# Group convolutions of a fused graph network: steps over the tiles that hold graphs (58), in place of four tiles in each of 16 batches

## The reference, cut to what matters

```python
GROUPS = [list(range(25)), [0, 1, 2, 3, 4, 5, 6, 7, 8], [0, 9, 10, 11, 12, 13, 14], [6, 7, 8, 12, 13, 14], [3, 4, 5, 9, 10, 11]]
def _graph_conv(x, adj, W, b):
    n = adj.shape[-1]
    A = adj + jnp.eye(n, dtype=adj.dtype)
    deg = jnp.sum(A, axis=-1)
    deg_safe = jnp.where(deg == 0, 1.0, deg)
    dinv = jnp.where(deg == 0, 0.0, deg_safe ** (-0.5))
    norm_adj = dinv[:, :, None] * A * dinv[:, None, :]
    support = jnp.einsum('bnd,de->bne', x, W)
    out = jnp.einsum('bnm,bme->bne', norm_adj, support) + b
    return jax.nn.relu(out)
...
    for g, idx_list in enumerate(GROUPS):
        idx = jnp.asarray(idx_list)
        x_g = x[:, idx, :]
        adj_g = adj[:, idx][:, :, idx]
        h = _graph_conv(x_g, adj_g, W1[g], b1[g])
        out_g = _graph_conv(h, adj_g, W2[g], b2[g])
        fused = fused.at[:, idx, :].add(norm_w[g] * out_g)
```

## Time and profile before

| | |
|---|---|
| time, median of 3 runs (lowest to highest) | 1251.85 us (1251.16 to 1252.07) |
| time of the profiled execution | 1249.13 us |
| its span, first to last instruction | 1247.3 us |
| mean granted TensorE clock | 0.937 of full speed |
| PE, DVE, ACT, POOL busy over the span | 91%, 82%, 78%, 61% |
| end of the first stage in the trace | 237.2 us |

### The profile page before, as it was taken

How to read it: one execution, slowest core, us unless ns; L and a number is a source line. 1 busy time by engine, 2 the same in 40 slices (tenths; PEclk the granted TensorE clock), 3 DMA queues, 4 the chain that set the end, 5 groups by cost and what they waited for, 6 DMA issues and landing times. The chain is left out here.

```text
span 1247.3 us, 20943 instructions
## 1 busy us (share of the span) xinstructions
PE 1141.1 (91%) x6346; PEld 862.7 (69%) x6346; DVE 1022.7 (82%) x3182; ACT 970.0 (78%) x1893; POOL 765.9 (61%) x693
## 2 busy tenths in 40 slices
PE   6889988559999999999999971899999999999998
PEld 4667766427888888888888861666666666676665
DVE  4678989896888888888888874788888888888875
ACT  3458766548999999999999971787877877878774
POOL 3346657547666666666666617776777767776620
PEclk9999985558999999999999995899999999999999
DMA  5579888103333333322333542232222232222310
GB/s 191 194 226 292 247 223 238 35 8 97 96 81 85 83 85 85 84 83 77 83 85 83 79 76 54 58 83 77 70 73 71 78 84 69 73 73 70 82 36 26
DMA packets 137475, 124.46 MB, mean 100 GB/s; under 512 B 14702, under 2 KB 116178, under 8 KB 136339
## 3 DMA queue, kind: packets, MB, share of 16 engines
q1 hardware_dynamic: 120083, 87.70, 23.1%
q0 software_dynamic: 17280, 35.42, 13.3%
HBM read 83.57 MB, written 39.50 MB: 99 GB/s over the span
## 5 line engine op out<-in xcount | busy, mean ns | idle before, releaser
L1092 POOL DMA_INDIRECT exg<-xln_scratch,ids x284 | 301.4, 1061 | 162.1 <-PE p_ex L1145 76.8
L1391 POOL DMA_INDIRECT yg<-expert_rows_scratch,pos_i x256 | 253.5, 990 | 96.9 <-issue 72.7
L1233 DVE TENSOR_TENSOR ehl<-ehr,ehh 128x512 fp32r<-128x512 f32 x284 | 194.2, 684 | 53.5 <-ACT ehh L1116 53.2
L1113 ACT ACTIVATE ehr<-p_eh,bc 128x512 f32<-128x512 f32 x284 | 196.1, 690 | 4.4 <-PE p_eh L1153 1.8
L1116 ACT ACTIVATE ehh<-ehr 128x512 fp32r<-128x512 f32 x284 | 179.7, 633 | 9.0
L1149 PE MATMUL p_eh<-exh,wh 128*128 128x512 f32 x284 | 124.4, 438 | 0.8 <-ACT exh L1107 0.8
L1398 POOL TENSOR_TENSOR root_l<-pre_l,mhalf 128x4 f32<-128x4 f32 x64 | 66.6, 1040 | 81.3 <-DVE pre_l L1665 80.5
L1158 PE MATMUL p_ey<-ehh,wh 128*128 128x512 f32 x284 | 112.0, 394 | 0.1
L1153 PE MATMUL p_eh<-exl,wh 128*128 128x512 f32 x284 | 111.9, 394 | 0.0
L1150 PE MATMUL p_eh<-exh,wl 128*128 128x512 f32 x284 | 111.9, 394 | 0.0
L1161 PE MATMUL p_ey<-ehl,wh 128*128 128x512 f32 x284 | 111.6, 393 | 0.0
(11 more groups left out here) (228 smaller groups left out, 2937.6 us busy)
## 6 DMA issues: line engine op xcount, KB each, us to landing
expert_rows_scratch<-eyo SPq DMA_DIRECT2D x71, 256.0 KB, 2.7
xtok<-in_x_tok SPq DMA_DIRECT2D x8, 1024.0 KB, 6.2
an<-in_a_t SPq DMA_DIRECT2D x16, 512.0 KB, 4.8
xln_scratch<-xl SPq DMA_DIRECT2D x16, 512.0 KB, 4.5
at<-in_a_t SPq DMA_DIRECT2D x32, 256.0 KB, 3.0
out<-outx SPq DMA_DIRECT2D x32, 256.0 KB, 2.6
wj<-in_w_grp SPq DMA_DIRECT2D x16, 321.0 KB, 4.3
exg<-xln_scratch,ids POOLq DMA_INDIRECT x284, 2.8
```

Of the source, the lines that this page charges most:

```text
L1092: pool.indirect_dma_start(out=xg[p][:, k, :], out_offset=None, in_=xln_d, in_offset=bass.IndirectOffsetOnAxis(ap=ids[:, R * j + k:R * j + ...
L1113: nc.scalar.activation(hr[c % 2][:, :], p_h[c][:, :], ACT.Relu, bias=bc[p][:, c:c + 1])\
L1233: nc.vector.tensor_tensor(hl[:, c, :], hr[c % 2][:, :], hh[:, c, :].bitcast(F32), ALU.subtract)\
L1391: pool.indirect_dma_start(out=yg[p][:, c, k, :], out_offset=None, in_=y_d, in_offset=bass.IndirectOffsetOnAxis(ap=pos_i[:, c, R * j + k:R ...
```

## The change

A list `full` says how many tiles of each batch hold graphs: 4 in turns 0 to 10 and 13, 3 for batches 11 and 12, 2 for batches 14 and 15. Loads, stores and the instructions of the group work take that many tiles. A loop over tiles gets shorter, and an instruction that covers a batch becomes narrower. The statistics, which take two tiles at once, have one instruction fewer for two tiles, and as many as before for three. The small tensors with one column per tile (`pre`, `root`, `nz`, `dinv`, `dsc`, `xsb`, `wdi`) are computed as before, with unused columns. Nothing is moved, and no wait or semaphore is added.

```diff
+            full = [min(R, -(-B // GPT[g]) - R * b) for g, b in order]
...
                     def load(j):
-                        sp.dma_start(xg[j % 2][:, :, :], x_grp[item[j]]).then_inc(loaded[j % 2], 16)
+                        n = full[j]
+                        sp.dma_start(xg[j % 2][:, 0:n, :], x_grp[item[j]][:, 0:n, :]).then_inc(loaded[j % 2], 16)
                         if j >= GA:
                             sp.wait_ge(o_done, j - GA + 1)
-                        sp.dma_start(ag[j % GA][:, :, :], a_grp[item[j]]).then_inc(loaded[j % 2], 16)
+                        sp.dma_start(ag[j % GA][:, 0:n, :], a_grp[item[j]][:, 0:n, :]).then_inc(loaded[j % 2], 16)
...
-                        sp.dma_start(dst, os_[j % 2][0:rows, :, :]).then_inc(rows_stored[j % 2], 16)
+                        sp.dma_start(dst, os_[j % 2][0:rows, 0:full[j], :]).then_inc(rows_stored[j % 2], 16)
...
-                        nc.gpsimd.tensor_tensor(ag[j % GA][:, :, :], ag[j % GA][:, :, :], plus, ALU.add)\
+                        tiles = ag[j % GA][:, 0:full[j], :]
+                        nc.gpsimd.tensor_tensor(tiles, tiles, plus(full[j]), ALU.add)\
                           .then_inc(ag_ready, 1)
...
-                            nc.scalar.activation(yt[:, :], p_y[:, :, :].rearrange("p r d -> p (r d)"), ACT.Copy)\
+                            nc.scalar.activation(yt[:, 0:full[t - 1] * P],
+                                                 p_y[:, 0:full[t - 1], :].rearrange("p r d -> p (r d)"), ACT.Copy)\
                               .then_inc(yt_ready, 1)
...
-                            for k in range(R):
+                            for k in range(full[t]):
                                 last = nc.scalar.activation(xs[p][:, k, :], xg[p][:, k, :], ACT.Identity,
                                                             scale=dsc[p][:, k:k + 1], bias=xsb[p][:, k:k + 1])
...
-                                nc.scalar.activation(ht[:, c, :], p_h[c][:, :], ACT.Relu,
+                                w = full[t - 1] * P
+                                nc.scalar.activation(ht[:, c, 0:w], p_h[c][:, 0:w], ACT.Relu,
...
-                            nc.scalar.activation(os_[p][:, :, :], os_[p][:, :, :], ACT.Relu).then_inc(orl_ready, 1)
+                            rows = os_[p][:, 0:full[t - 2], :]
+                            nc.scalar.activation(rows, rows, ACT.Relu).then_inc(orl_ready, 1)
...
-                            for k in range(R):
+                            for k in range(full[t]):
                                 last = nc.tensor.matmul(p_deg[:, k:k + 1], ag[t % GA][:, k, :], ones[:, :],
...
-                            for k in range(R):
+                            for k in range(full[t - 1]):
                                 last = nc.tensor.matmul(p_y[:, k, :], ag[(t - 1) % GA][:, k, :], xs[q][:, k, :],
...
-                            for k in range(R):
+                            for k in range(full[t - 2]):
                                 for c in range(2):
                                     last = nc.tensor.matmul(p_z[:, k, :], ht[:, c, k * P:(k + 1) * P],
...
-                                nc.tensor.matmul(p_h[c][:, :], wj[q][:, c * P:(c + 1) * P], yt[:, :],
+                                w = full[t - 1] * P
+                                nc.tensor.matmul(p_h[c][:, 0:w], wj[q][:, c * P:(c + 1) * P], yt[:, 0:w],
...
-                            for k in range(0, R, 2):
+                            for k in range(0, full[t], 2):
                                 last = two_rows(st[p][:, k:k + 2, :], xg[p][:, k:k + 2, :])
...
-                            nc.vector.tensor_tensor(ys[:, :, :], p_y[:, :, :],
+                            n = full[t - 1]
+                            nc.vector.tensor_tensor(ys[:, 0:n, :], p_y[:, 0:n, :],
...
-                            nc.vector.tensor_tensor(zs[:, :, :], p_z[:, :, :],
+                            n = full[t - 2]
+                            nc.vector.tensor_tensor(zs[:, 0:n, :], p_z[:, 0:n, :],
...
-                            for k in range(R):
+                            for k in range(full[t - 2]):
                                 last = nc.vector.scalar_tensor_tensor(os_[p][:, k, :], p_z[:, k, :],
```

More of the change, by code:

```diff
@@ L321, in store @@
                         rows = GPT[g] * GN[g]
-                        dst = c_d[g][b * R * rows:(b + 1) * R * rows, :].rearrange("(k r) d -> r k d", r=rows)
+                        dst = c_d[g][b * R * rows:(b * R + full[j]) * rows, :].rearrange("(k r) d -> r k d", r=rows)
                         sp.wait_ge(orl_ready, j + 1)
-                        sp.dma_start(dst, os_[j % 2][0:rows, :, :]).then_inc(rows_stored[j % 2], 16)
+                        sp.dma_start(dst, os_[j % 2][0:rows, 0:full[j], :]).then_inc(rows_stored[j % 2], 16)
                     def load_rows(i):
@@ L394, in _ @@
                     pool.wait_ge(id_loaded, 16)
-                    plus = ident.unsqueeze(1).to_broadcast([P, R, P])
+                    plus = lambda n: ident.unsqueeze(1).to_broadcast([P, n, P])
                     def add(j):
                         pool.wait_ge(loaded[j % 2], 32 * (j // 2) + 32)
-                        nc.gpsimd.tensor_tensor(ag[j % GA][:, :, :], ag[j % GA][:, :, :], plus, ALU.add)\
+                        tiles = ag[j % GA][:, 0:full[j], :]
+                        nc.gpsimd.tensor_tensor(tiles, tiles, plus(full[j]), ALU.add)\
                           .then_inc(ag_ready, 1)
@@ L661, in _ @@
                             dve.wait_ge(y_done, t)
-                            nc.vector.tensor_tensor(ys[:, :, :], p_y[:, :, :],
-                                                    dinv[(t - 1) % GA][:, :].unsqueeze(2).to_broadcast([P, R, D]),
+                            n = full[t - 1]
+                            nc.vector.tensor_tensor(ys[:, 0:n, :], p_y[:, 0:n, :],
+                                                    dinv[(t - 1) % GA][:, 0:n].unsqueeze(2).to_broadcast([P, n, D]),
                                                     ALU.mult).then_inc(ys_ready, 1)
@@ L704, in _ @@
                             dve.wait_ge(z_done, t - 1)
-                            nc.vector.tensor_tensor(zs[:, :, :], p_z[:, :, :],
-                                                    dinv[(t - 2) % GA][:, :].unsqueeze(2).to_broadcast([P, R, D]),
+                            n = full[t - 2]
+                            nc.vector.tensor_tensor(zs[:, 0:n, :], p_z[:, 0:n, :],
+                                                    dinv[(t - 2) % GA][:, 0:n].unsqueeze(2).to_broadcast([P, n, D]),
                                                     ALU.mult).then_inc(zs_ready, 1)
```

## The result

| | before | changed |
|---|---|---|
| median of 7 runs | 1251.16 us | 1243.60 us |
| lowest to highest | 1246.68 to 1252.07 | 1242.01 to 1246.19 |
| profiled execution, its span | 1249.13, 1247.3 us | 1242.01, 1240.2 us |
| start of the routing stage in the trace | 237.2 us | 229.9 us |

The ratio is 0.9944 with a 95% interval of 0.9931 to 0.9958, so the change gains 5 to 9 us. 1245.4 us had been forecast. In a later set of runs the same kernel had a ratio of 0.9955 (0.9941 to 0.997). From the routing stage to the end the trace has 1240.2 - 229.9 = 1010.3 us against 1247.3 - 237.2 = 1010.1 before. All of the difference lies in the first stage.

A forecast was written before the change was run, and what follows sets the result against it. DVE was taken to bound the first stage until about turn 14, then PE; 7.1 us gained at `p_sel` of turn 18 less 0.7 for landings gave 6.4 us, hence 1242.7 profiled and 1245.4 us median, range 1241.8 to 1249.6.

The forecast's parts named there:

- who sets the pace: First stage, turns 11 to 17: DVE sets the pace until about turn 14, PE in turns 15 to 17.
- interval 11: Interval t ends at the `os` issued in turn t; in 11, one degree product less before DVE's wait saves 0.24 us.
- POOL holds DVE: DVE instructions stay stretched until POOL's addition ends; shorter additions release them sooner, some 0.56 us of it in interval 14.
- the two statistics instructions: Turns 14 and 15: dropping one of 0.37 us each gains nothing, since L649 behind them ends with `deg_sums` on POOL.
- 17: `os` 0.56, `zs` 0.33, wait 1.46: 2.35: Interval 17 loses 2.35 us: shorter `os` and `zs` on DVE, and the wait for PE before `os`.
- the transfers as a rival: Transfers bind: intervals 16 and 17 stay above 7.5 us, `ct` lands late, gain only 3 to 4.5 us; chance 0.10.
- PE's chain ... sets the end of the stage: Token turns from turn 18: PE's chain, with ACT's copies between, uses up its lead and sets the stage's end.
- the figure of 2.6 us per full-clock stretch: Token turns: a 3.3 us stretch at full clock was estimated to save some 2.6 us of PE's chain.
- the rival that rested on it: Clock in the token turns: 2.6 to 4 us lost, chance 0.12, or about 1242.5 us if better, chance 0.09.
- The 6.4 us: Total gain at the end of the first stage: 7.1 us at `p_sel` of turn 18 less 0.7 for later landings.
- Wrong if the granted clock falls before the last `os`: Sign of failure: PE's clock should not fall during the group turns, before the last `os`.
- The slower rival: PE's clock falls inside group turns 15 to 17: 17 us lost against 6.4 won, 1262 us; chance 0.04.

The follow-up runs named there:

- run 1: Changed kernel with only PE following the tiles that hold graphs, everything else handling four tiles; 1247.75 us, ratio 0.9985 to the kernel before.
- run 2: Changed kernel with PE working on four tiles in every batch, everything else following the tiles that hold graphs; 1246.99 us, ratio 0.998.
- run 3: Changed kernel, but POOL adds the identity to all four places of the adjacency; 1246.21 us, ratio 0.997.
- run 4: Changed kernel, but the statistics of batches 14 and 15 take both pairs of tiles again; 1242.73 us, ratio 0.995.
- run 11: Changed kernel with ct loads ahead of the xl store from turn 15 on, and eight extra PE products in turns 18 to 23; 1242.04 us, ratio 0.9934.
- run 8: The changed kernel again, with no edit and a second profile; 1248.70 us, ratio 0.9955.
- run 5: Changed kernel with SP issuing the next turn's ct loads before the store of xl in each turn; 1248.01 us, ratio 0.995.
- run 7: Changed kernel with ct loads before the xl store in each turn, and eight extra PE products per turn from turn 18; 1249.94 us, ratio 0.9954.
- run 10: Changed kernel with eight extra PE products per turn in turns 18 to 23 alone; 1243.03 us, ratio 0.9937.
- run 12: Changed kernel, but loads and stores move four tiles in every batch again; 1243.39 us, ratio 0.9942.
- run 9: Changed kernel with ct loads ahead of the store of xl only from turn 15 on; 1240.09 us, ratio 0.9915.
- run 6: Changed kernel with eight extra 128x128 products per turn on PE from turn 18, in front of p_sel; 1247.66 us, ratio 0.9947.

## Why the prediction held, and which of its steps did not

**Right: who sets the pace.** Runs 1 and 2 take the change apart as the forecast did. DVE sets intervals 13 and 14, with PE close behind, and PE the waits before `os` in 15 and 16. Of the sum, interval 11 gave 0.2 (0.24 forecast), 12 gave 0.4 (0, at most 0.45), 13 without a fall of the clock 1.0 (0.9), 14 gave 1.1 (1.1), 15 gave 0.9 (1.06), 16 gave 2.3 (2.4).

**Right: POOL holds DVE.** Run 3 shows the 0.56 us of interval 14, and run 4 that the two statistics instructions are worth nothing. In interval 13 the size was right and the way to it was not: the shorter `ys` brought DVE to L687's successor by the time POOL began, which was 0.1 us later behind `root`, so the stretched instruction of the earlier trace rows was not shortened but passed by. (In runs 4 and 11 that successor was caught itself, for 0.76 and 0.77 us in place of 0.28.) The columns were priced a little high: `ys` takes 0.55 us for three tiles and 0.42 for two, so that a tile is 0.13 and not 0.165.

**Failed: "17: `os` 0.56, `zs` 0.33, wait 1.46: 2.35".** It was -0.6 in the first profile, 0.2 in run 8. The step took the wait for PE away and did not ask what PE would wait for next. It was `ct`: SP issues it behind the store of `xl`, which waits for ACT. PE was ready for `p_sel` of turn 17 at 158.25 us, 8.6 us sooner than before, but the first `ct` issue had moved by only 4.1 us (158.16 to 154.06), and PE came before it had landed. The profiles after the change line up by this wait (us; runs 1 and 2 are left out, where PE or DVE do other work):

| run | wait for `ct` in turn 17 | interval 17 | clock in it |
|---|---|---|---|
| 5, 7 (`ct` ahead) | 0, 0 | 6.5, 6.5 | full |
| 4 | 0.33 | 6.5 | full |
| 11 (`ct` ahead) | 0.67 | 6.8 | full |
| 10 | 1.39 | 7.8 | half in the last 0.9 |
| 3 | 1.47 | 7.9 | half in the last 0.2 |
| 12 | 2.10 | 8.7 | half in the last 1.3 |
| 9 (`ct` ahead) | 0 | 7.3 | half in the last 2.8 |
| 6 | 2.12 | 9.0 | half in the last 1.7 |
| 8 | 1.06 | 8.6 | half in the last 3.8 |
| changed, first profile | 1.84 | 9.4 | half in the last 4.9 |

Interval 17 is 6.45 us, which the forecast had (6.4), plus the wait, plus up to 1.1 us where it ran at half clock for long. So of the 3.0 us missing in the first profile 1.8 are the wait and about 1.1 the clock. That the wait brings the clock down is not shown: in run 9 the clock fell without one, and in run 10 it stayed up through a wait of 1.39 us and fell 1.1 us behind it. The forecast had the transfers as a rival, by bandwidth. Run 9 speaks against that, since its interval 17 moved 284 GB/s without a wait, and so does run 12, whose extra 1.17 MB cost nothing in the median; it is the order of SP's queue.

**Failed: "PE's chain ... sets the end of the stage".** DVE sets turns 18 to 23, at either clock: it is busy for 6.7 of the 7.18 us of a turn and waits 0.2 of the rest for POOL, and the turn lasts as long at a clock of 0.50 as at 0.74 (the windows above) and at full (run 10). `gnb` starts 6.3 us sooner than before in each of them. PE's chain is worth only DVE's waits in the last turns, 3.4 us in the earlier trace rows, 2.1 in the changed kernel and 0.9 in run 10, but 0.9 in runs 4 and 9 too, which have no extra products. So the figure of 2.6 us per full-clock stretch, and with it the rival that rested on it, was mis-sized: half clock in the token turns costs at most some 2.5 us in all, not 2.6 for every 3 us.

**So the total was right partly by compensation.** The 6.4 us did not run through interval 17 but through `xl`, `ct` and `p_sel` of turn 18. Up to there the path held: `xl` and the first `ct` issue of turn 17 came 7.9 us sooner (164.95 to 157.06, 168.64 to 160.75), 6.9 without the 1.0 us of turn 3, and 7.1 had been reckoned. Then the path was another. PE, late from interval 17, came to `p_sel` straight from its logits at 167.46 us and did not wait for `ct`. That is 6.6 us sooner, 5.6 without turn 3, where 6.4 us and 167.7 had been forecast. The 1.0 us of turn 3, by chance of the execution, and 1.0 us in the last turns made up for it. The medians lay 7.6 us below before in the first set and 5.1 us in that of run 8.

**By its own signs the mechanism failed in part.** "Wrong if the granted clock falls before the last `os`": it fell twice, at 124.2 us for 3.4 us and at 158.4 for 6.8. A wait for `ct` above a microsecond came in turn 17, not in turn 16. The end of the stage moved by as much as `p_sel` of turn 18, and more. The clock falls at least once before the last `os` in every profile, that of before (at 86.5 us) included, and up to four times (runs 1, 3 and 9). A fall of 3.4 us in intervals 13 to 16 costs 0.7 to 1.3 us: interval 13 is 10.9 us with one (changed kernel, run 8) and 10.2 without (runs 6 and 11).

**The slower rival** was seen in small: in run 1, where PE lost work and DVE did not, the clock fell for 6.8 and 3.4 us, intervals 13 and 14 grew by 0.6 and 1.1 us, and it rose again by itself. In the changed kernel, where both engines lose work, the two falls ended by themselves as well. That thinner work on PE causes them is not shown: the kernel before has the same fall elsewhere.

## What to carry to other kernels

When an engine stops being waited for, look up what it will wait for itself, down to the position of the transfer in the issuing queue: here 1 to 2 us of the gain lay in five DMA issues that stood behind a store. Moving them ahead, only where no load stands behind them, gave some 3 us more in one pair of medians (runs 9 and 12) and an unclear 1 us in another (runs 11 and 10). Cutting padding pays where all engines that share the pace get it together; each half alone gave a third. Before a stall is called the bound of a later stage, make its cause go away for once: a stage at half clock looked bound by PE and was not.

## What the runs showed of the hardware

**A later transfer can be faster.** In turn 3, before any changed instruction, the trace of before has:

```profile
33.12 1.27 POOL L399 TENSOR_TENSOR ag<-ag,cf 128x512 f32<-128x512 f32 x1 [0.27 <-DMA ag<-in_a_grp]
33.16 1.25 DVE L697 TENSOR_TENSOR dsc<-dinv,root 128x4 f32<-128x4 f32 x1
```

and the trace of after:

```profile
33.11 0.16 DVE L706 TENSOR_TENSOR dsc<-dinv,root 128x4 f32<-128x4 f32 x1
...
33.51 0.69 DVE L715 TENSOR_TENSOR zs<-p_z,dinv 128x512 f32<-128x512 f32 x1
33.73 1.27 POOL L403 TENSOR_TENSOR ag<-ag,cf 128x512 f32<-128x512 f32 x1 [0.92 <-DMA ag<-in_a_grp]
```

The adjacency landed 0.6 us later, POOL began later, and a DVE instruction on 128x4 elements was not caught behind it: 0.16 us in place of 1.25. By the rule of the Trainium skill (SBUF — State Buffer, Who interferes with whom) a DVE instruction with two SBUF inputs contends with a GpSimd instruction that reads SBUF, for a port pair that only one of them can hold at a time. The trace agrees: the stretched row of before ends within 0.02 us of POOL's. The turn is 1.0 us shorter for a transfer 0.6 us late.

**The clock fell behind a busy PE.** In the changed kernel it fell at 124.2 us, 0.5 us after the end of the logits, which are products of eight columns each and had run for 1.9 us:

```profile
118.00:124.00 6.00, 5.80 (x50) 5.40 (x48) 5.87 (x23) 4.87 (x12) 4.24 (x4) 1.00 0.83 275
124.20:127.50 3.30, 3.30 (x10) 1.72 (x10) 2.54 (x12) 2.06 (x5) 1.76 (x2) 0.50 0.92 273
```

PE had been busy for 5.80 of 6.00 us. The prediction had argued from the share in which PE is busy that the clock would stay up in these turns. That argument does not hold.
